# Projected heads two slots sooner on TensorE and inside VectorE's search, in a fused Perceiver block on one core

## What is computed

```python
x = x + _L0_xattn_ref(ctx_1024, ctx_1024, _layernorm(x), mask, Wv, Wk, Wq, Wo, bo)
x = x + _L0_attn_ref(_layernorm(x), Wq, bq, Wk, bk, Wv, bv, Wo, bo)

# _L0_xattn_ref: 16 heads of 16 values, 256 queries against 4096 keys
energy = jnp.einsum('nqhd,nkhd->nhqk', q, k)
attn = jax.nn.softmax(energy * (1.0 / E ** 0.5), axis=3)
out = jnp.einsum('nhqk,nkhd->nqhd', attn, v).reshape(N, Sq, E)
return out @ Wo.T + bo

# _L0_attn_ref: 16 heads, 256 keys, only the 64 largest scores of a row count
scores = jnp.einsum('bhqd,bhkd->bhqk', q, k) / scale
top_scores, top_idx = jax.lax.top_k(scores, TOP_K)
w = jax.nn.softmax(top_scores, axis=-1)
```

## Time and profile before

| | before |
|---|---|
| median of 3 runs | 1630.84 us (1628.27 to 1631.99) |
| the profiled execution | 1630.52 us, of it a span of 1629.0 us |
| TensorE busy | 1393.0 us (86% of the span) |
| VectorE busy | 1302.9 us (80%) |
| ScalarE busy | 996.6 us (61%) |
| GpSimd busy | 274.1 us (17%) |
| mean granted TensorE clock | 0.911 of full speed |

### The profile page before, as it was taken

One profiled execution on the slowest core, in us unless ns is written; L12 is line 12 of the kernel. 1 busy time (PEld: TensorE's weight loads), 2 busy tenths in 40 slices (PEclk: granted clock), 3 DMA queues, 4 the chain that ended last, 5 costly groups with the idle time before them and its releaser, 6 DMA issues. The chain is left out here.

```text
span 1629.0 us, 31741 instructions
## 1 busy us (share of the span) xinstructions
PE 1393.0 (86%) x11858; PEld 871.6 (54%) x11858; DVE 1302.9 (80%) x3920; ACT 996.6 (61%) x1627; POOL 274.1 (17%) x253
## 2 busy tenths in 40 slices
PE   8999899999999998999977797698868869777756
PEld 4555456665665665666654484376346426433423
DVE  1221169999798998989988999998996897897993
ACT  5778667777677776777753443276475566554540
POOL 4110012222222222223222221221100100010000
PEclk9999989999899999999988899789879988796777
DMA  7755322444032203302105122115345346233230
GB/s 151 161 118 130 67 59 73 92 92 92 15 54 53 28 27 54 53 8 47 40 1 173 52 79 78 52 53 161 122 115 154 111 119 159 62 83 105 72 84 7
DMA packets 96855, 132.64 MB, mean 81 GB/s; under 512 B 20195, under 2 KB 80875, under 8 KB 93747
## 3 DMA queue, kind: packets, MB, share of 16 engines
q1 hardware_dynamic: 96688, 130.50, 32.6%
HBM read 124.95 MB, written 5.51 MB: 80 GB/s over the span
## 5 line engine op out<-in xcount | busy, mean ns | idle before, releaser
L1365 ACT ACTIVATE attn_arena<-ps 128x1024 f32<-128x1024 f32 x512 | 497.2, 1024 | 203.9 <-PE ps L425 198.2
L1966 DVE MATCH_REPLACE8 attn_late<-attn_top,attn_late 128x256 f32<-128x256 f32 x1024 | 422.5, 432 | 0.0
L1963 DVE MAX8 attn_top<-attn_late 128x8 f32<-128x256 f32 x1024 | 391.4, 434 | 22.3 <-ACT attn_late L1387 22.3
L425 PE MATMUL ps<-attn_arena 32*128 32x256 f32 x4096 | 375.2, 408 | 10.7 <-ACT attn_arena L1365 6.6
L425 PEld LDWEIGHTS ps<-attn_arena 32*128 32x128 f32 x4096 | 253.9, 188 | 79.3 <-issue 41.2
L439 PE MATMUL ps<-attn_arena 128*32 128x256 f32 x4096 | 280.7, 391 | 4.2 <-issue 3.5
L1252 POOL TENSOR_SCALAR attn_late<-attn_late 128x512 f32<-128x512 f32 x64 | 95.6, 1494 | 602.8 <-DVE attn_late L1966 602.8
L439 PEld LDWEIGHTS ps<-attn_arena 128*32 128x32 f32 x4096 | 108.5, 110 | 137.8 <-issue 78.3
L700 PE MATMUL ps<-attn_arena 128*128 128x256 f32 x512 | 133.7, 408 | 22.0 <-ACT attn_arena L1467 21.9
L1512 ACT ACTIVATE attn_arena<-attn_late,attn_arena 128x255 f32<-128x255 f32 x256 | 108.6, 499 | 71.2 <-DVE attn_late L1797 44.8
L678 PE MATMUL ps<-attn_arena,attn_q 128*128 128x512 f32 x256 | 135.2, 660 | 13.9 <-ACT attn_arena L1453 13.7
(11 more groups left out here) (241 smaller groups left out, 1675.0 us busy)
## 6 DMA issues: line engine op xcount, KB each, us to landing
attn_arena<-ctxT SPq DMA_DIRECT2D x124, 256.0 KB, 4.7
attn_arena<-maskT SPq DMA_DIRECT2D x32, 512.0 KB, 4.5
attn_arena<-ctx SPq DMA_DIRECT2D x32, 512.0 KB, 4.2
attn_late<-rows SPq DMA_DIRECT2D x256, 64.0 KB, 2.3
attn_arena<-ctxV SPq DMA_DIRECT2D x15, 1024.0 KB, 13.2
attn_late<-wide SPq DMA_DIRECT2D x64, 128.0 KB, 3.0
attn_early<-wide SPq DMA_DIRECT2D x64, 128.0 KB, 3.4
wide<-attn_early SPq DMA_DIRECT2D x16, 256.0 KB, 2.8
```

The lines of the kernel that those rows point to most:

```text
L425: mm = pe.matmul(ps[:, first + j - 2 * i, u * S:(u + 1) * S], kx[n % 2][rows, k0:k0 + P], qpad[rows, n % GROUPS, b * S:(b + 1) * S], start ...
L1365: act.activation(probs[m % 2][:, 2 * i:2 * i + 2], ps[:, first:first + 2, :], ACT.Exp, scale=1.0 / 16.0).then_inc(exp_done, 1)
L1963: dve.max(top[:, t, turn], s[:, i, t] if turn == 0 else work[:, i, t]).then_inc(picked, 1)
L1966: dve.match_replace(work[:, i, t], top[:, t, turn], s[:, i, t] if turn == 0 else work[:, i, t], LOW).then_inc(picked, 1)
```

## The change

Pieces of four engines move, and no instruction is added or taken away.

- ScalarE copies the turned heads straight behind its branch (slot 0 of d = 1) and not behind `take_pT` in slot 1.
- TensorE runs `project` in slot 1 of d = 1, not slot 3.
- VectorE's add and normalisation stand before turn 5 of step d = 1, not before turn 0 of step d = 2. GpSimd's root and the bias that follows move from d = 2 to d = 1, past one `keep_top`.
- In d = 2, `turn_x`, `make_qk` and the first `scores` each stand one slot earlier on TensorE, and ScalarE's copies with them.

```diff
@@ tensor, slots 0 to 3 @@
                         if ending and d == 1:
                             turn_heads(h, m if m is not None else CROSS_ITS - 1)
+                        if ending and d == 2:
+                            turn_x(h)
                     if slot == 1:
                         if 0 <= p + 1 < B * H and (p + 1) % H:
                             scores(p + 1)
                         if ending and d == 0:
                             turn_acc(h, GROUPS - 1)
+                        if ending and d == 1:
+                            project(h)
                         if ending and d == 2:
-                            turn_x(h)
+                            make_qk(h, 0)
                     if slot == 2:
                         if 0 <= done < B * H:
                             products(done)
                         if ending and d == 2:
-                            make_qk(h, 0)
+                            scores(p + 1)
                     if slot == 3:
...
-                        if ending and d == 1:
-                            project(h)
-                        if ending and d == 2:
-                            scores(p + 1)
@@ scalar @@
                             nc.switch_bb(f"scalar_usual{h}")
+                            take_misc(headsT.rearrange("p c s -> p (c s)"), M_, "heads", h)
+                        if ending and d == 2:
+                            take_misc(xnT.rearrange("p c s -> p (c s)"), M_, "xn", h)
                     if slot == 1:
                         if 0 <= done < B * H:
                             take_pT(done)
-                        if ending and d == 1:
-                            take_misc(headsT.rearrange("p c s -> p (c s)"), M_, "heads", h)
                         if ending and d == 2:
-                            take_misc(xnT.rearrange("p c s -> p (c s)"), M_, "xn", h)
+                            take_qk(h, 0)
                     if slot == 2:
-                        if 0 <= p + 1 < B * H and (p + 1) % H:
+                        if 0 <= p + 1 < B * H:
                             take_scores(p + 1)
-                        if ending and d == 2:
-                            take_sums(done) if done >= 0 else None
-                            take_qk(h, 0)
@@ vector @@
-                if turn == 0 and ending and d == 2:
+                if turn == 5 and ending and d == 1:
                     dve.wait_ge(bo0_added, h + 1)
                     add(h, "projected")
                     normalise(norms[0], X[:, h * T:(h + 1) * T], xn).then_inc(xn_ready, 1)
```

More of the change, by code:

```diff
@@ L1589, in _ @@
                             take_misc(general[:, h:h + 1], M_[:, 0:1], "bad", h)
-                        elif ending and d == 2:
-                            take_scores(p + 1)
                         elif 0 <= done < B * H:
```

## The result

The changed kernel takes 1646.4 us (median of 4 runs, 1640.0 to 1650.1) against 1630.2 of the kernel before beside it. The ratio is 1.0102, with a 95% interval of 1.0081 to 1.0123. A second measurement gave 1.0077 (1.0053 to 1.0101). The forecast was 1632.0 and the range ended at 1638: slower had been given a chance of 0.25. The profiled execution took 1640.0 us (span 1638.5), the fastest of the four, 9.5 us more than the one before.

A forecast was written before the change was run, and what follows sets the result against it. TensorE and VectorE were both taken as full between batches, the later deciding at each boundary. Batch terms -1.0, -(3.4 - S), +(1.6 + S) and +0.3 gave +1.1 us with S = 1.8, so 1632; range 1625.5 to 1638.

The forecast's parts named there:

- Mid-search waits of VectorE: VectorE would wait 4 to 6 us before the add in the middle of a search, three times, not at its end.
- TensorE waiting about 4 us for GpSimd: At `turn_pm`, new waits for `keep_top`: about 4 us at some 423 and 651, and 5 us at 870.
- the forecast's 427.2 and 416.1: Batch 1: VectorE's add could go on at 416.1 and GpSimd's `keep_top(14)` would be done at 427.2, making TensorE wait.
- The 1.16 us: TensorE's wait of 1.16 us for ScalarE at the boundaries of batches 1 and 2, forecast to go away.
- S: What a slow TensorE clock costs behind a new wait at `turn_pm`: taken as 1.8 us, bounds 0 and 3.3.
- a clock of 0.5 for 3 to 4 us: Profile sign of S: TensorE's clock at half speed behind its new waits; a full clock would mean S = 0.
- Batch 1's stretch v0 to v1: Batch 1's boundary, between the values' adds of batches 0 and 1: forecast 3.4 - S us earlier.
- Batch 2: Batch 2's boundary: TensorE, which sets the pace, reaches the next `turn_pm` 1.6 + S us later.
- Batch 3: Batch 3's boundary, where TensorE has room: 0.3 us later, or 1.9 if a later wait took nothing back.
- Batch 0: Batch 0's boundary, with no `turn_pm` in the way: 1.0 us earlier, at least 0, at most 3.
- -2.5 + 2S: Sum over the four batch boundaries, S charged at batches 1 and 2: +1.1 us with S = 1.8.
- the wait breeds more: Rival: TensorE's waits keep the clock down through the next step and batch 3 keeps 1.9: +5.7 us, 1636.5; chance 21%.

The follow-up runs named there:

- e1: The changed kernel again with no edit, beside fresh runs of the kernel before: 1645.5 us, ratio 1.0077.
- e2: Changed kernel with VectorE's add and normalisation and GpSimd's root put back behind the search (turn 0 of d = 2): 1630.5 us, ratio 0.9988.
- e14: Changed kernel, order kept, with heads 14 and 30 searching only 8 columns in turns 5 to 7, so the new wait goes: 1632.4 us, ratio 1.0004.
- e15: Changed kernel with the add before turn 6 instead of turn 5; new wait 1.56 us: 1630.8 us, ratio 1.0005.
- e17: Kernel before with the change for batch 1 alone, the add before turn 7 instead of turn 5: 1630.0 us, ratio 1.0001.
- e3: Kernel before with the whole change made for batch 1 alone: 1644.6 us, ratio 1.0069.
- e10: Changed kernel with heads 20 and 28 searching only 8 columns in their last turns, removing the old waits: 1633.4 us, ratio 1.0021.
- e9: Kernel before with heads 20 and 28 searching only 8 columns in their last turns, removing the old waits: 1626.8 us, ratio 0.9994.
- e4: Kernel before with the whole change made for batch 2 alone, so unchanged up to 640 us: 1639.4 us, ratio 1.0034.
- e12: Changed kernel with the add and normalisation before turn 7 instead of turn 5: 1620.8 us, ratio 0.9945.

## Why the prediction was wrong

**Right: the moves of time.** Mid-search waits of VectorE: three of 4 to 6 us forecast, 5.08, 6.69 and 3.20 found, so all three there and two just outside the sizes. "TensorE waiting about 4 us for GpSimd": 3.00 and 3.00, and 5.32 where 5 was said. `keep_top(14)` ended at 421.83 + 1.27 = 423.10, 11.2 us behind the add's start; the forecast's 427.2 and 416.1 are 11.1 apart. The 1.16 us are gone. VectorE's wait before head 16 was to be under 3.26: 2.92. The one before head 32 was to grow: 1.10 to 1.39.

**Nearly right: S, right behind the wait.** From `turn_pm` to head 16's scores TensorE took 433.95 - 423.15 = 10.80 us at batch 1 and 670.71 - 662.59 = 8.12 at batch 2, with the same instructions. So S was 2.7 and 0, where 1.8 was taken twice; the bounds 0 and 3.3 held both. The sign named for it, a clock of 0.5 for 3 to 4 us, was not seen at either: 6.8 us and none.

**Nearly right: the sum without the later heads.** Batch 1's stretch v0 to v1 took 222.6 to 223.0 us in the four profiles with the new wait, and 224.2 in the mean of seven profiles with the boundary as before (221.8 to 226.1): 1.3 faster, forecast 1.6. (The one pair above has +1.1, since the profile before is one of the two fastest there.) Batch 2: +6.3 less the 5.2 of the old wait at 624, so +1.1 where 3.4 was forecast (its S was 0). Batch 3, from v2 to the end: +0.2 in this pair, forecast +0.3. Over the four profiles with this part as forecast and the ten with batch 3 as before it is +2.2: the stretch behind v3 takes 727.3 to 732.2 us where it took 725.4 to 726.6, a cost that the sum has no term for. Batch 0 can't be read from one pair of profiles: v0 came between 224 and 239 us in those with the move and between 231 and 236 in those without.

There is a second way to this number. Within the runs of one kernel the time falls by 1.38 us for each 0.001 of mean clock (a line through 312 runs of all versions, each taken from its own kernel's mean). By that, 11.6 of e1's 14.3 us in the mean go with the clock and 2.7 are left, where the forecast was +1.1. It is a correlation, and shows no cause by itself.

**Wrong: where the slow clock is charged.** The step that failed is the sum's last line, "-2.5 + 2S": it charges the slow clock twice, right behind each new wait, up to the next scores. The bounds of S were drawn from stretches that end there. The old waits at 512 and 621 did not move and so had no term, although are such a wait; with 20.5 and 17.1 us of low clock behind them, and not 3.4 and 3.4, they cost 12.1 us in the profiled run. The rival "the wait breeds more" had the right side and named the clock, but let it stay low "through the next step"; it was back at 428.9, and low again 79 us later. Nothing in the sum could give more than +5.7.

**Shown and not shown.** Shown: the usual loss comes with the new wait of batch 1 and goes with it (e2, e14, e15, e17 against e1 and e3), and by the ratios two thirds of it need the old waits at 508 and 621 (e10 less e9). Shown in the profiles: it is time at the low level with TensorE busy. Not shown: how a wait of 3 us makes the clock stay low behind another wait 80 us later, and why the same kernel does so in some runs and not in others. The 6.8 us of low clock right behind the new wait do not explain it, since the kernel before has as much at that boundary, a little later, and only 3.4 us at 512:

```profile
430.00:437.00 7.00, 7.00 (x36) 4.81 (x32) 7.00 (x30) 2.06 (x4) 0.00 (x0) 0.52 0.00 1
```

No run here could set the clock's state by hand, or keep the wait and move VectorE alone.

## What to carry to other kernels

Where TensorE's clock can fall, do not price a new wait by itself. A hole of 3 us cost 11 to 15 us here, by the runs most of it behind two older waits that nobody had touched; with a hole of 1.6 us the kernel was as fast as before. So when work is moved into another engine's search, put it where nothing that TensorE waits for stands behind it: one or two turns behind the add cost nothing that can be told, three did. And when runs of one kernel differ by 20 us, compare the low stretches of several profiles, and tell two versions apart by a dozen runs each: the first pair of profiles had batch 0 5.2 us faster and batch 1 1.1 slower, and neither held.

## What the runs showed of the hardware

- The low clock can last 17 to 20 us with TensorE busy throughout, where it lasted 3.4 us behind the same wait in other versions. e4's profile shows it with the instructions of the kernel before.
- The same wait of 2.57 us was followed by no fall of the clock (e12), by 3.4 us (before), by 17.1 (e4) and by 20.5 us (changed); a wait of 3.00 us at 662 by none, one of 3.00 us at 423 by 6.8 (both changed).
- The mean clock of one program differs between its runs by 0.01 and more (0.901 to 0.917 in one version), and the time with it: 1618 to 1643 us (e12).
